# A pipelined transformer kernel: a copy moved from ScalarE to VectorE, TensorE's loop placed 18 slots later, and two score blocks issued in halves

## The reference, cut to what matters

```python
def attn_layer(x, Wqkv, qs, ksc, Wo):          # 16 heads of 64, windows of 32
    q, k, v = heads(x @ Wqkv)
    q = l2norm(q) * qs; k = l2norm(k) * ksc
    q = q * cos * scale + rotate_half(q) * sin * scale
    k = k * cos * inv + rotate_half(k) * sin * inv
    out = local_attention(q, k, v)             # own window and the one before
    return out @ Wo
def ffn_layer(x, g, bln, W1, b1, W2, b2):
    xn = layernorm(x) * g + bln
    a, gate = split(xn @ W1 + b1)
    return a * gelu(gate) @ W2 + b2
for i in range(6):
    x = attn_layer(shift_tokens(x), ...) + x
    x = ffn_layer(shift_tokens(x), ...) + x
```

## Time and profile before

| | us |
|---|---|
| median of three executions | 4722.76 |
| lowest, highest | 4708.98, 4727.22 |
| the profiled execution, its own time | 4691.7 |
| its span, first to last instruction | 4689.9 |
| PE busy, DVE busy, ACT busy, POOL busy (share of the span) | 85%, 68%, 66%, 18% |
| mean granted clock of TensorE | 0.962 |

### The profile page before, as it was taken

The page is one execution under the profiler, slowest core; times in us unless marked ns, Lnnn a source line. Parts: engine busy times, 40 slices in busy tenths (PEclk is TensorE's granted clock), DMA queues, the critical chain, the costliest instruction groups (busy, mean ns, idle before and its releaser), DMA issues. The chain is left out here.

```text
span 4689.9 us, 172910 instructions
## 1 busy us (share of the span) xinstructions
PE 3973.2 (85%) x68188; PEld 2844.2 (61%) x68188; DVE 3168.6 (68%) x6779; ACT 3110.2 (66%) x8351; POOL 867.3 (18%) x1240
## 2 busy tenths in 40 slices
PE   7968888888888888888888888888888888885678
PEld 4746666666666666666666666666666666663334
DVE  4856776666667666666767666666766676665665
ACT  4836776777777677777767777776777777672233
POOL 0012122122121212112122112121211212110122
PEclk9979999999999999999999999999999999996689
DMA  0034344444334444334444434434444443430000
GB/s 28 1 80 83 75 83 83 87 88 85 77 77 80 96 88 83 79 74 83 92 88 80 82 78 86 92 78 81 83 83 91 82 81 77 80 74 17 3 5 12
DMA packets 126144, 336.58 MB, mean 72 GB/s; under 512 B 32592, under 2 KB 33744, under 8 KB 125264
## 3 DMA queue, kind: packets, MB, share of 16 engines
q0 software_dynamic: 61440, 201.38, 23.6%
q1 hardware_dynamic: 64080, 125.25, 10.6%
HBM read 22.41 MB, written 2.10 MB: 5 GB/s over the span
## 5 line engine op out<-in xcount | busy, mean ns | idle before, releaser
L1173 ACT ACTIVATE loc_probs<-loc_pair,loc_ebias,loc_rnorm 128x64 f32<-128x64 f32 x3072 | 1201.2, 434 | 9.7 <-DVE loc_ebias L1333 7.3
L919 PE MATMUL loc_pair<-loc_hs,loc_wqk 128*128 128x256 f32 x3072 | 748.9, 387 | 27.7 <-issue 19.5
L1173 ACT ACTIVATION_READ_ACCUMULATOR loc_probs<-loc_pair,loc_ebias,loc_rnorm 128x1 f32 x3072 | 723.9, 236 | 0.0
L919 PEld LDWEIGHTS loc_pair<-loc_hs,loc_wqk 128*128 128x128 f32 x3072 | 567.3, 192 | 128.4 <-issue 42.6
L1331 DVE TENSOR_REDUCE loc_mx<-loc_pair 128x8 f32<-128x512 f32 x384 | 264.8, 689 | 469.5 <-PE loc_pair L965 466.6
L868 POOL DMA_DIRECT2D loc_ks<-loc_msin x384 | 331.5, 1008 | 1230.2 <-DVE loc_msin L1281 1193.8
L1155 ACT ACTIVATE loc_sq<-loc_pair 128x1024 f32<-128x1024 f32 x384 | 397.2, 1034 | 211.5 <-PE loc_pair L919 211.5
L868 POOL DMA_DIRECT2D loc_qr<-loc_msin x384 | 332.1, 1006 | 1079.1 <-DVE loc_msin L1281 1061.4
L1281 DVE SCALAR_TENSOR_TENSOR loc_msin<-loc_pair,loc_scal,loc_tab 128x1024 f32<-128x1024 f32 x384 | 490.1, 1276 | 2.1 <-DMA loc_ks<-loc_msin 2.1
L965 PE MATMUL loc_pair<-loc_kr,loc_qr 64*32 64x64 f32 x24576 | 311.0, 226 | 121.8 <-issue 121.8
L965 PEld LDWEIGHTS loc_pair<-loc_kr,loc_qr 64*32 64x32 f32 x24576 | 263.3, 106 | 220.2 <-issue 219.9
(11 more groups left out here) (232 smaller groups left out, 7271.8 us busy)
## 6 DMA issues: line engine op xcount, KB each, us to landing
loc_ks<-loc_msin POOLq DMA_DIRECT2D x384, 256.0 KB, 4.5
loc_qr<-loc_msin POOLq DMA_DIRECT2D x384, 256.0 KB, 5.1
loc_veven<-loc_vodd SPq DMA_DIRECT2D x768, 64.0 KB, 3.5
loc_veven<-loc_vodd SPq DMA_DIRECT2D x384, 128.0 KB, 3.9
loc_wqk<-wqk_dram SPq DMA_DIRECT2D x12, 512.0 KB, 4.2
loc_wv<-wv_dram SPq DMA_DIRECT2D x6, 512.0 KB, 5.9
loc_wo<-wo_dram SPq DMA_DIRECT2D x6, 512.0 KB, 3.5
x<-xT_dram SPq DMA_DIRECT2D x1, 2048.0 KB, 7.4
```

Of the source, the lines that this page charges most:

```text
L919: ins = nc.tensor.matmul(pairs[b][:, p // 2, (p % 2) * UNIT:(p % 2 + 1) * UNIT], wqk[:, k, w:w + P], hs[u.odd][:, :], start=True, stop=True)
L1173: ins = nc.scalar.activation(probs[x][:, p, hp, :], pairs[b][:, hp, p * 2 * WIN:(p + 1) * 2 * WIN], ACT.Exp, bias=ebias[x][:, k:k + 1], sc ...
```

## The change

It has three parts. `norms_out` goes from ACT's program to DVE's, between `rotate_sin(3)` and `norms_in`; `reciprocals(0)` goes ahead of `norms_in`. The first instruction of TensorE's loop goes from slot 208 to slot 226 of a block. In the step with `odd` 0, the 64 matmuls of `scores(1)` are issued as 32, then `project(3)`, then 32; those of `scores(0)` as 32, then `outputs_across(0)` and `spread(1)`, then 32. `sim_ps` is raised after the second half. In the step with `odd` 1 the order is as before. `weighted` gets the same argument, but no caller uses it.

```diff
             for s in range(FILL):
-                step(filling(s))
+                step(filling(s), s % 2)
             with nc.Fori(FILL // 2, TOTAL // 2, engines=bass.OrderedEngineSet([eng.engine]), hint_back_edge=True,
-                         head_slot={eng.engine: 208} if eng is nc.tensor else None) as i:
+                         head_slot={eng.engine: 226} if eng is nc.tensor else None) as i:
                 for odd in range(2):
-                    step(lambda k: Unit(2 * i + (odd - k), (odd - k) % 2))
+                    step(lambda k: Unit(2 * i + (odd - k), (odd - k) % 2), odd)
...
+            half_or_all = lambda parts: range(PAIRS // 2 * parts[0], PAIRS // 2 * (parts[-1] + 1))
...
-            def scores(x, u, b):
+            def scores(x, u, b, parts=(0, 1)):
                 if u is None:
                     return
-                after(pe, kr_ready, u.n, 2, x + 1)
-                after(pe, ktail, u.n)
-                for i in (2, 3):
-                    landed(pe, i, u.n)
-                    own_wait(pe, passed)
-                for hp in range(2):
+                if 0 in parts:
+                    after(pe, kr_ready, u.n, 2, x + 1)
+                    after(pe, ktail, u.n)
+                    for i in (2, 3):
+                        landed(pe, i, u.n)
+                        own_wait(pe, passed)
+                for hp in range(2 if 0 in parts else 0):
...
-                for p in range(PAIRS):
+                for p in half_or_all(parts):
...
-                ins.then_inc(sim_ps, 1)
+                if 1 in parts:
+                    ins.then_inc(sim_ps, 1)
...
+            whole = (0, 1)
...
-                    scores(1, at(3), 2)
+                    scores(1, at(3), 2, whole if odd else (0,))
                 if at(2) is not None:
                     vacated(pe, ((oT_ready, at(4), 2, 2), (exp_ready, at(3), 4, 2), (rot, at(2), 8, 2),))
                     project(3, at(2), 1)
+                if not odd:
+                    scores(1, at(3), 2, (1,))
...
-                    scores(0, at(2), 1)
+                    scores(0, at(2), 1, whole if odd else (0,))
                 if at(3) is not None:
                     vacated(pe, ((probsT_ready, at(3), 2, 2),))
                     outputs_across(0, at(3), 2)
                 if at(2) is not None:
                     vacated(pe, ((rot, at(1), 8, 4), (v_ready, at(3), 2, 2),))
                     spread(1, at(2), 0)
+                if not odd:
+                    scores(0, at(2), 1, (1,))
...
-            def norms_out(u, b):
-                if u is None:
-                    return
-                after(act, norm_ps, u.n)
-                after(act, nT_ps, u.n - 1)
-                nc.scalar.activation(nT[:, :], bank(b)[:, 0:UNIT], ACT.Copy).then_inc(nT_ready, 1)
...
-                norms_out(at(2), 4)
                 exponentials(1, 0, at(3), 2)
...
+            def norms_out(u, b):
+                if u is None:
+                    return
+                after(dve, norm_ps, u.n)
+                nc.vector.tensor_copy(nT[:, :], bank(b)[:, 0:UNIT]).then_inc(nT_ready, 1)
...
                 rotate_sin(3, at(2), 1)
+                norms_out(at(2), 4)
+                reciprocals(0, at(3))
                 norms_in(at(2), 4)
-                reciprocals(0, at(3))
                 newton(at(2))
```

More of the change, by code:

```diff
@@ L885, in ffn_params, with step @@
                 nc.gpsimd.tensor_copy(fpar[u.odd][:, :], params[:, bass.ds(u.layer, 1), 2:NPAR].rearrange("p l k -> p (l k)")).then_inc(fpar_ready, 1)
-            def step(at):
+            def step(at, odd):
                 halves_across(0, at(2))
@@ L989, in probs_across, with weighted @@
                 ins.then_inc(probsT_ps, 1)
-            def weighted(x, u, b):
+            def weighted(x, u, b, parts=(0, 1)):
                 if u is None:
                     return
[L994 to L997, removed]
+                if 0 in parts:
+                    after(pe, probsT_ready, u.n, 2, x + 1)
+                    after(pe, veven_ready[x], u.n, VMOVE, VMOVE)
+                    own_wait(pe, passed)
+                for p in half_or_all(parts):
                     for w in range(4):
@@ L1004, in weighted @@
                                                    start=True, stop=True, tile_position=(hp * DH, WIN * w))
-                ins.then_inc(pv_ps, 1)
+                if 1 in parts:
+                    ins.then_inc(pv_ps, 1)
             def outputs_across(x, u, b):
```

## The result

| us | before | after |
|---|---|---|
| median | 4719.11 (4 runs) | 4793.42 (4 runs) |
| lowest, highest | 4708.98, 4727.22 | 4787.79, 4802.94 |
| span of the profiled execution | 4689.9 | 4801.1 |
| mean granted clock of TensorE | 0.962 | 0.932 |

The changed kernel is slower: ratio 1.0161, 95% interval 1.0133 to 1.0188. Forecast were 4783 and, as likeliest direction, slower. The profiled execution of before (span 4689.9) lies under all times of the table and that of after (4801.1) is the slowest of its own, so that the two traces stand 111 us apart and the medians 74. What follows explains the 111 of the traces by turns; between kernels the ratios of their runs are used.

What follows compares the result with a forecast made beforehand. TensorE bounds the kernel, waiting for its own instructions in the first step. First step -0.95, second -0.55, return +3.0: +1.5 us a turn, about +60 in all, 4752; plus 31 for the median, 4783. Own range 4735 to 4830, overall 4615 to 4850.

Steps and rivals of the forecast that it cites:

- What bounds the kernel: TensorE's first step: stops in small matmuls are waits for its own instructions at 256-slot boundaries, 0.5 to 1.9 us at five.
- Rival 2: Stops at block boundaries: crossings mostly hidden, so the change's second and third parts would be worth nothing; chance 0.07.
- The return: Loop's branch back on TensorE: it lands in block 12, whose late fetch costs 3.0 us a turn, bounds 0 and 3.4.
- Rival 1: At the return: the head's block still comes in time, costing nothing; -1.5 us a turn, 4648; chance 0.32.
- The clock behind the return: TensorE after the return: a lower clock in every turn, 1.5 us, counted only in rival 3.
- rival 3: DVE bounds the first step and the clock drops after each return: +3.0 us a turn, about 4851; chance 0.12.
- The copy: The norms copy leaving ACT, ahead of its table load and exponentials: 0.55 us off each step, 0.18 waiting and 0.38 copying.
- The first step: First step of a turn: +1.35 - 1.88 - 0.4 = -0.95 us, bounds -2.3 and +0.5.
- `weighted(0)`: First step, not split: still stops near its end, 18 slots earlier; delay +1.35 us instead of +1.45.
- The maxima later by 2.4: DVE, first step: scores end 2.4 us later, so maxima, rotations and then `loc_nT` come later.
- The second step: Second step of a turn: no instruction stops before, only the copy counts, -0.55 us.
- rival 4: Larger gains: first step -2.0 us, return 2.5, no net change, near 4725; chance 0.09.

## Why the prediction was right, and where it was not

**What bounds the kernel: right.** All stops that the forecast took for instruction fetches moved with the head by the slots, at 208, 218, 226 and 168, and the return jumped between two neighbouring slots. The packets say the same: in the trace of before, each of the four stops inside blocks of the first step ends 1.1 to 1.6 us after an instruction packet has ended, in all 45 turns. Rival 2 is ruled out by the two kernels, and by the 13 packets in a turn. So the Trainium skill's sentence (Runtime: NRT & Kernel Launch, Instruction fetch mechanics) that a crossing is "mostly hidden" does not hold in front of blocks of small matmuls. The same section's rule that a taken branch to a target outside two pages waits for a fetch doesn't tell the runs at 218 and 219 apart: the head lies more than ten blocks behind the branch in both, and the return costs 0.58 or 5.03.

**The return (forecast 3.0 us, bounds 0 and 3.4): right in kind, too small.** Measured +4.11, and above the upper bound. The row on the way out of the loop (2.54) priced a block that follows in order. Here, in the 44 returns, the head's packet begins 1.2 to 2.5 us after the branch does, takes 0.9 to 1.8, and the projection begins 2.0 us after it has ended. Rival 1 had a chance of 0.32 and falls.

**The clock behind the return: given to rival 3 only, at 1.5 us a turn.** It happens in every turn, for 1.8 us in the mean. This half of rival 3 was true.

**The copy (0.55 us a step): missed by 0.4.** The run alone gives 87 us, the list of waits of ACT 0.93 a step. Two turns stood for ninety-six.

**The first step (forecast -0.95, measured -1.41): near by errors that cancel.**
- "The stop in `weighted(1)` comes after 3 passes and ends when the block arrives, as now": wrong, it goes. Behind the long return block 1 is there in time: a stop of 0.54 to 0.71 in `ln_var` is what is left.
- "The stop in `scores(1)`, 0.85 us, goes: the projection between the halves gives the block 2 us": it goes, but by the head; the projection isn't needed at 226.
- `weighted(0)`: "+1.35 instead of +1.45"; it was 1.95 in the mean and is 0.73. Here too one turn stood for all.
- The maxima later by 2.4: they came 2.0 later in the mean, counted from `project(2)`, but by other parts than the sum's. The slower work behind the return brings 1.8 and the projection 1.9; the stops that went take back 1.7. The victim was wrong. I followed the delay to `loc_nT`, behind the rotations. But DVE's gate stands between the maxima and the rotations, and PE's sums of squares take the bank that the gate reads. Timeline of DVE in the changed kernel:

```profile
2078.38 0.69 DVE L1341 TENSOR_REDUCE loc_mx<-loc_pair 128x8 f32<-128x512 f32 x1 [5.36 <-PE loc_pair L968]
...
2081.52 0.48 DVE L1411 SCALAR_TENSOR_TENSOR loc_act_out<-loc_one,loc_fpar,loc_gelu 128x256 f32<-128x256 f32 x1
...
2085.49 0.42 DVE L1293 COPY loc_nT<-loc_one 128x256 f32<-128x256 f32 x1 [1.10 <-PE loc_one L929]
```

The gate ends at 2082.00, and `norms` begins at 2082.14. Before, that wait was 0.17 us in the mean. It costs 2.1 us, and another 0.8 in the mean by the clock behind it (0.63 in this turn, the lower level in 23 of 45). With the wait gone (scores(0) alone in halves, at 208) the clock there is full in all 45.

In sum of the table above, 6.5 us of idle time went from the first step (the six stops and waits of the rows `weighted(1)` to `scores(0)` other than the sums of squares, less the 0.73 left in `weighted(0)`, and 0.21 ahead of `probs_across(0)`), 2.7 came (the sums of squares 1.93, `ln_var` 0.58, the masks 0.22), and the time in which PE stood in no such wait grew by 2.3 in the mean (1.7 in the projection, 0.8 behind the sums of squares' wait, 0.3 in `ln_var`, less 0.5 elsewhere): by busy time, in the turns shown, 37.32 against

```profile
2060.65:2104.03 43.38, 39.47 (x689) 28.49 (x690) 24.73 (x53) 26.01 (x66) 7.65 (x11) 0.91 0.35 68
```

Together -1.5, measured -1.4.

**The second step (forecast -0.55, measured -0.13).** The copy alone brought 0.83 there and the head alone cost 0.79, together -0.04. Of the 0.79, block 12 takes 0.51 by its stop one pass before the end of `spread(1)` (0.47 in the changed kernel); the forecast put all of this block into the return.

The total was closer than its parts, and that is luck. By the traces a turn costs 2.57 us more where the sum had 1.5: return and clock were 2.9 us too low, and a copy worth some 0.8 more in a turn and stops that left the first step by themselves made up for most of it. By the medians 4783 stands against 4793 only because the two profiled executions lie further apart than the medians do. Some figures of the prediction don't follow from its own terms, with at most 3 us in 4783: the return was counted 45 times and comes 44 times, rival 4's terms give 4714 and not 4725, and the terms of the forecast's own range give 4721 to 4838 and not 4735 to 4830.

## What to carry to other kernels

Where TensorE stops inside blocks of small matmuls with "issue" as the releaser, divide the slot numbers by 256 before looking for a semaphore. The place of the loop's head is then a parameter like any other; in this loop the branch must not fall into a thirteenth block (4.2 us a turn). Work put between two halves of a block hides the next instructions, but its price is the delay of the block's reader: look at every bank that this engine releases later in its order, not only at the next data. And price a wait from the list of waits over all turns, never from one turn.

## What was not expected of the hardware

- One slot further (218 to 219) cost 189 us in 45 turns; the return went from 0.58 to 5.03 us.
- Removing the instruction that names the branch made the kernel at 226 0.9% faster, and at 208 only 0.7% slower, with one packet more in a turn: the instruction saves 2.1 us in the return there and gives 1.4 back in the first step. Why a first step behind it has larger stops stays open.
- The sizes of the stops at 168 came out as 2.9 us after the 64th slot of a block, a figure fitted to the stops of before and of the runs at 208: 1.14, 1.77 and 0.62 measured where 1.1, 1.8 and 0.8 were expected. That the next block is asked for there is an inference from these times; no row shows the request itself.
- A gap of 4.5 us on TensorE was followed by the lower clock in all 44 turns (0.58 over the next 5.5 us in the mean, the projection 3.7 us against 1.99); the wait of 2.1 us ahead of the sums of squares in 23 of 45 turns, and with the head at 208 in 20 of 45; the return of 2.61 us in 18 of 44, with no order by length (low behind one of 2.01 us, full behind one of 3.17); the gap of 1.2 us in `weighted(1)` of the kernel before in none of 45.
- The branch of TensorE's loop takes 1.42 us in the median in the kernel before and 4.61 in the changed one; the same branch on VectorE, ScalarE and GpSimd takes 0.05 to 0.06.
